# Half of a softmax's row sums as identity products on TensorE, a sorting router, and new orders in a fused adaLN block

## The reference, cut to what matters

```python
h = _rmsnorm(x, norm_w)
v = (h @ W_v.T).reshape(B, T, H, M)                         # H = 8, M = 16
gates = jax.nn.softmax((h @ W_a.T).reshape(B, T, H, M, M + 1), axis=-1)
a0, A = gates[..., 0], gates[..., 1:]
# over the 512 tokens, one after another:
new = jnp.einsum('bhij,bhj->bhi', A_t, state) + (a0 * v)_t
return x + h_out @ W_out.T
```

```python
logits = x @ router_weight.T + router_bias                  # 8 experts
topk_logits, topk_idx = jax.lax.top_k(logits, 4)            # softmax over the four, else 0
act = (clip(up, -7, 7) + 1) * gate * sigmoid(1.702 * gate)  # gate = minimum(gate, 7)
y = sum over experts of combine[expert] * (act @ down_proj.T + bias)
```

## Time and profile before

| | us |
|---|---|
| median of 3 runs | 792.42 |
| the three runs | 788.27, 792.42, 794.17 |
| profiled execution, its own time | 789.0 |
| its span, first to last instruction | 787.3 |
| VectorE busy | 678.0 (86%) |
| TensorE products busy | 589.9 (75%) |
| GpSimd busy | 567.5 (72%) |
| ScalarE busy | 552.2 (70%) |

### The profile page before, as it was taken

One profiled execution on the slowest core, in us unless ns is written; L12 is line 12 of the kernel. 1 busy time (PEld: TensorE's weight loads), 2 busy tenths in 40 slices (PEclk: granted clock), 3 DMA queues, 4 the chain that ended last, 5 costly groups with the idle time before them and its releaser, 6 DMA issues.

```text
span 787.3 us, 12543 instructions
## 1 busy us (share of the span) xinstructions
PE 589.9 (75%) x2826; PEld 441.0 (56%) x2826; DVE 678.0 (86%) x2921; ACT 552.2 (70%) x1272; POOL 567.5 (72%) x635
## 2 busy tenths in 40 slices
PE   5785144787968697877878686979788785878986
PEld 3242022565746475665657474757666574757875
DVE  4569999999999999999999999999989999888331
ACT  4764142777786878787777878786867776657885
POOL 2685556687878797888878787978878686735554
PEclk9886565899999999999999999998989997889998
DMA  6265645453726455364537273644545463720000
GB/s 189 83 145 139 139 116 137 102 130 83 171 79 149 107 122 120 79 159 81 129 95 160 77 159 97 134 115 116 117 79 122 108 141 86 163 71 8 14 8 7
DMA packets 162234, 85.34 MB, mean 108 GB/s; under 512 B 77752, under 2 KB 156784, under 8 KB 157936
## 3 DMA queue, kind: packets, MB, share of 16 engines
q1 hardware_dynamic: 162160, 84.55, 46.3%
HBM read 44.66 MB, written 39.85 MB: 107 GB/s over the span
## 4 chain that ended last, share of the span: by engine, by line
DVE 66%; PE 14%; issue 10%; ACT 5%; POOL 3%; DMA 1%; SPq 1%; POOLq 0%; ACTq 0%; DVEq 0%
DVE ps L854 15%; DVE prod L846 14%; DVE ps L860 8%; DVE act_t L926 7%; DVE nmax L824 6%; DVE zs L831 6%; PE ps L1184 6%; PE ps L1197 4%; DVE rz L837 3%; PE ps L1171 2%; ACT ex L590 1%; ACT ps L624 1%; POOL ex L414 1%; ACT up L618 1%; DMA gates<-gate_dram 1%
## 5 line engine op out<-in xcount | busy, mean ns | idle before, releaser
L1184 PE MATMUL ps<-h2t,wgu 128*128 128x256 f32 x1024 | 256.4, 393 | 24.6 <-ACT up L618 24.6
L1184 PEld LDWEIGHTS ps<-h2t,wgu 128*128 128x128 f32 x1024 | 192.6, 196 | 71.4 <-ACT up L618 29.8
L1171 PE MATMUL ps<-wl,ht 128*128 128x512 f32 (+1 forms) x320 | 168.4, 629 | 71.5 <-ACT lg L601 67.6
L1197 PE MATMUL ps<-wd,act_t 128*128 128x128 f32 x1024 | 146.5, 288 | 65.7 <-DVE act_t L926 65.6
L1197 PEld LDWEIGHTS ps<-wd,act_t 128*128 128x128 f32 x1024 | 135.3, 200 | 95.4 <-DVE act_t L926 84.9
L854 DVE TENSOR_REDUCE ps<-prod 128x8 f32<-128x136 f32 x512 | 152.5, 298 | 10.6
L846 DVE TENSOR_TENSOR prod<-gates,ps 128x136 f32<-128x136 f32 x512 | 147.1, 287 | 14.7 <-DMA gates<-gate_dram 6.4
L421 POOL TENSOR_TENSOR lg<-lg,nmax 128x1088 f32<-128x1088 f32 x64 | 130.3, 2039 | 15.0 <-DVE nmax L824 13.1
L676 ACT ACTIVATE weighted<-ps,comb 128x128 f32<-128x128 f32 x256 | 79.9, 363 | 85.4 <-PE ps L1197 83.1
L461 POOL TENSOR_SCALAR up<-up 128x512 f32<-128x512 f32 x128 | 78.4, 612 | 79.3 <-ACT up L618 75.2
L414 POOL TENSOR_TENSOR ex<-ex,rz 128x1088 f32<-128x1088 f32 x64 | 129.2, 2039 | 8.8 <-DVE rz L837 5.7
(11 more groups left out here) (122 smaller groups left out, 586.0 us busy)
## 6 DMA issues: line engine op xcount, KB each, us to landing
gate_dram<-ex SPq DMA_DIRECT2D x256, 136.0 KB, 3.3
gates<-gate_dram SPq DMA_DIRECT2D x32, 1088.0 KB, 5.5
yt_tok<-y_dram SPq DMA_DIRECT2D x256, 8.0 KB, 3.4
xg<-in_L_attn_x_dram SPq DMA_DIRECT2D x32, 64.0 KB
y_dram<-ys SPq DMA_DIRECT2D x32, 64.0 KB, 2.0
out_dram<-res_out SPq DMA_DIRECT2D x32, 64.0 KB
wa_rows<-in_L_attn_W_a_dram SPq DMA_DIRECT2D x1, 1088.0 KB, 5.7
dn_rows<-in_L_ffn_down_proj_dram SPq DMA_DIRECT2D x1, 1024.0 KB, 12.3
```

The lines of the kernel that those rows point to most:

```text
L1171: nc.tensor.matmul(ps[:, n % 2, 0:w], ht[:, g % RH, j * P:(j + 1) * P], wl[:, k * LC:k * LC + w], start=True, stop=True).then_inc(lg_ps.se ...
L1184: last = nc.tensor.matmul(gu_ps(m, k, which)[:, q * N:(q + 1) * N], wgu[:, k, rows + q * P:rows + (q + 1) * P], h2t[:, m % 2, :], start=Tr ...
L1197: last = nc.tensor.matmul(dn_ps(j), act_t[:, k % 2, q * N + j * P:q * N + (j + 1) * P], wd[:, k, q, :], start=(q == 0), stop=(q == KI - 1))
```

## The change

The row sums of the second tile of a chunk leave VectorE. TensorE adds the 17 columns of every row instead: 17 products with the identity as weights, which accumulate in one of the two banks of the logits; the sum takes one turn among the logits (11 turns for each chunk and not 10). The reciprocal of this tile reads the bank. The product with v no longer waits for the reciprocal's sums on VectorE but for TensorE.

The scan's product leaves out the first column, whose factor was 1, and is written in place over the gates; `prod` and the state's column of ones go. The router sorts the 8 logits (`max`), overwrites the four lower of the sorted list by 2^127, and lets `match_replace` mark the four upper in the logits; its small tensors are in SBUF. `mean_term` goes to GpSimd as a product and a negation. Stores of gates and loads of states are 4 transfers of two batches each. `up`, `act_t` and `weighted` have three buffers. The orders of VectorE's slots, ScalarE, GpSimd and TensorE are changed.

```diff
+        def item_bank(c, i):
+            return ps[:, (ITEMS * c + i) % 2, :]
+        def lg_bank(g, n):
+            return item_bank(g, n if n < SUM_AT else n + 1)          # SUM_AT = 4, ITEMS = 11
+        def zs_bank(e):
+            return item_bank(e + 1, SUM_AT)[:, 0:HI]
...
+            def row_sums(e, part):
+                if part == 0:
+                    wait_item(pe, e + 1, SUM_AT - 2)
+                    pe.wait_ge(exp_ok.sem, exp_ok.at(e, 2))
+                v = ex[:, 1, :].rearrange("p (r k) -> p r k", k=M1)
+                cuts = (0, 6, 12, M1)
+                for k in range(cuts[part], cuts[part + 1]):
+                    last = nc.tensor.matmul(zs_bank(e), ident[:, :], v[:, :, k], start=(k == 0), stop=(k == M1 - 1))
+                if part == 2:
+                    last.then_inc(zs_ps.sem, 1)
...
+                    dve.wait_ge(zs_ps.sem, zs_ps.at(e, 1))
+                    nc.vector.reciprocal(rz[:, j, :], zs_bank(e)).then_inc(rz_ok.sem, 1)
...
-                nc.vector.tensor_tensor(
-                    prod[:, :].rearrange("p (i k) -> p i k", k=M1),
-                    gates[:, t, :].rearrange("p (i k) -> p i k", k=M1),
-                    state[:, (t - 1) % TS, :].unsqueeze(1).broadcast_to([P, HALF, M1]), ALU.mult).then_inc(scan.sem, 1)
+                own = gates[:, t, :].rearrange("p (i k) -> p i k", k=M1)[:, :, 1:M1]
+                nc.vector.tensor_tensor(own, own, state[:, (t - 1) % TS, :].unsqueeze(1).broadcast_to([P, HALF, M]),
+                                        ALU.mult).then_inc(scan.sem, 1)
...
+                elif n == 1:
+                    dve.wait_ge(rank_in.sem, rank_in.at(p, 1))
+                    for j in range(TILES):
+                        nc.vector.max(top[:, j, :], rl[:, j, :]).then_inc(rank_in.sem, 1)
+                elif n == 2:
+                    dve.wait_ge(rank_in.sem, rank_in.at(p, 3))
+                    nc.vector.tensor_tensor(rdl[:, :, :], rl[:, :, :], top[:, :, 0:1].broadcast_to([P, TILES, E]),
+                                            ALU.subtract).then_inc(rank_in.sem, 1)
+                    nc.vector.memset(top[:, :, TOP_K:E], BIG).then_inc(rank_in.sem, 1)
+                else:
+                    for j in range(TILES):
+                        nc.vector.match_replace(out=left[:, j, :], in_to_replace=top[:, j, :], in_values=rl[:, j, :],
+                                                imm_value=-BIG).then_inc(rank_in.sem, 1)
...
+                    nc.vector.scalar_tensor_tensor(out=rsl[:, :, :], in0=left[:, :, :], scalar=-BIG, in1=rex[:, :, :],
+                                                   op0=ALU.is_equal, op1=ALU.mult).then_inc(weigh.sem, 1)
...
+            def mean_term(mv, rs, rs_ok, nm, nx_ok, nm_ok, c):       # in GpSimd's block
+                nc.gpsimd.tensor_tensor(nm[:, :, 0], mv[:, :, 0], rs[:, :, 0], ALU.mult).then_inc(nx_ok.sem, 1)
+                nc.gpsimd.tensor_scalar(nm[:, :, 0], nm[:, :, 0], -1.0, 0.0, ALU.mult, ALU.add).then_inc(nm_ok.sem, 1)
...
-                for b in range(B):
-                    sp.dma_start(gate_dram[j, b // 2, :, b % 2].rearrange("r t e -> t r e"),
-                                 ex[b * TS:(b + 1) * TS, j, :].rearrange("p (r e) -> p r e", e=ROW)
+                for q in range(B // 2):
+                    sp.dma_start(gate_dram[j, q].rearrange("r b t e -> (b t) r e"),
+                                 ex[2 * TS * q:2 * TS * (q + 1), j, :].rearrange("p (r e) -> p r e", e=ROW)
                                  ).then_inc(g_st[j].sem, 16)
```

More of the change, by code:

```diff
@@ L231, in adaln_block @@
         y_st = [event(f"y_st{j}", 16) for j in range(TILES)]
-        y_ld = [event(f"y_ld{j}", 16 * B) for j in range(TILES)]
+        y_ld = [event(f"y_ld{j}", 16 * B // 2) for j in range(TILES)]
         yt_ps, yt_ok, o_ps = event("yt_ps", 1), event("yt_ok", 1), event("o_ps", 1)
@@ L475, in run @@
             def run(a, g, e, s, p, m, o):
+                if o is not None:
+                    finish(o)
+                if m is not None:
+                    clamp_up(m, 0)
                 if a is not None:
@@ L533, in run @@
                     inv_sqrt(ms[:, :, 0], eps_sum, me, rms, me_ok, rms_ok, a)
+                if m is not None:
+                    accumulate(m, 6)
                 if g is not None:
@@ L685, in run @@
                     logits_out(g, 0)
+                if o is not None:
+                    weigh_expert(o, E - 1)
                 if e is not None:
@@ L698, in run @@
                     combine_out(m)
+                    up_and_silu(m, 1)
+                    bias_out(m)
+                if a is not None:
+                    squares(a)
+                if m is not None:
                     weigh_expert(m, 0)
@@ L1033, in between @@
                     if p is not None:
                         second_stats(p, 0)
-                elif u == 57:
-                    if p is not None:
                         second_stats(p, 1)
-                elif u == 59:
+                        for j in range(TILES):
+                            aggregate(st2, mv2, st2_ok, mv2_ok, p, j)
+                elif u == 60:
                     if m is not None:
                         hidden(m, 3)
-                elif u == 60:
-                    if p is not None:
-                        for j in range(TILES):
-                            aggregate(st2, mv2, st2_ok, mv2_ok, p, j)
-                elif u == 66:
+                elif u == 61:
@@ L1067, in between @@
                     if p is not None:
                         router_ranks(p, 0)
-                elif u == 84:
+                elif u == 88:
                     if p is not None:
                         router_ranks(p, 1)
-                elif u == 88:
+                elif u == 91:
                     if p is not None:
                         router_ranks(p, 2)
-                elif u == 89:
+                elif u == 93:
+                    if m is not None:
+                        hidden(m, 7)
+                elif u == 95:
@@ L1260, in run @@
                     logits(g, 0)
+                    logits(g, 1)
                 if m is not None:
                     gate_up(m, 0)
-                if g is not None:
-                    logits(g, 1)
-                if m is not None:
                     gate_up(m, 1)
@@ L1272, in run @@
                     logits(g, 3)
+                if e is not None:
+                    row_sums(e, 0)
+                    row_sums(e, 1)
+                    row_sums(e, 2)
+                if m is not None:
+                    down(m, 0)
+                if g is not None:
                     logits(g, 4)
                 if m is not None:
-                    down(m, 0)
                     down_bias(m)
-                    gate_up(m, 2)
                 if g is not None:
@@ L1285, in run @@
                     gate_up(m, 3)
-                if g is not None:
-                    logits(g, 6)
                 if p is not None:
@@ L1290, in run @@
                 if g is not None:
+                    logits(g, 6)
                     logits(g, 7)
@@ L1293, in run @@
                     down(m, 2)
+                    gate_up(m, 4)
                 if g is not None:
                     logits(g, 8)
+                    logits(g, 9)
                 if m is not None:
-                    gate_up(m, 4)
-                if g is not None:
-                    logits(g, 9)
+                    down(m, 3)
+                    gate_up(m, 5)
                 if a is not None:
@@ L1302, in run @@
                 if m is not None:
-                    down(m, 3)
-                    gate_up(m, 5)
                     down(m, 4)
```

310 lines of the change are left out of this document (123 added, 187 removed).

## The result

The changed kernel takes 863.24 us, the median of four runs (858.91 to 863.94), beside 792.96 for the kernel before (788.27 to 794.17). The ratio is 1.087, with a 95% interval of 1.083 to 1.092: slower by 70 us, where 15 us less was predicted, and far over the range's upper end of 804. Its profiled execution has a span of 861.3 us at a mean granted clock of 0.923; before it was 787.3 at 0.917. They can differ by up to 0.4% from the quotients of the medians printed; that of the kernel before is 790.25 in twelve runs beside the experiments.

What follows compares the result with a forecast made beforehand. VectorE bounds the kernel. Twelve iterations go from 43.16 to 42.2 us, saving 11.5; -11.5 + 1.5 - 1.5 - 1.5 = -13 on the span of 787.3 gives 774.3, as a median 777; range 750 to 804.

Steps and rivals of the forecast that it cites:

- What bounds the kernel: Steady iteration of 42.86 us: VectorE, busy 41.17 in 43 us, sets the pace, with the other engines close behind.
- VectorE's own sum: VectorE's time per steady iteration without new waits for other engines: 42.86 - 2.0 - 0.27 - 0.4 + 0 + 0.3 = 40.5 us.
- locks: Three router instructions of VectorE with two SBUF inputs wait for GpSimd: 1.5 us an iteration, bounds 0 and 4.
- The scan's product and the mean terms: VectorE, per iteration: 128 elements instead of 136 save 0.27 us, mean terms moved to GpSimd save 0.4.
- net 0: Router on VectorE: new small instructions cost 0.6 us an iteration, as the old ones did; bounds -0.3 and +0.8.
- The identity sums: TensorE's 17 products with the identity, 0.22 us each, 3.8 an iteration; the reciprocal at slot 30 waits about 1.
- the identity sums are late: Rival, chance 0.14: stride or low clock doubles the sums' cost on TensorE, giving 806 us.
- Logits(3) starts near 9.4 and ends at 10.2: TensorE's fourth logits product, just ahead of the sums, starts 9.4 us into the iteration, not 10.75; sums end at 14.0.
- The two overlap rather than add: The reciprocal's wait of about 1 us and the locks' 1.5 an iteration overlap, since late locks give TensorE time.
- 42.0 with the locks: Forecast steady iteration: VectorE's own sum of 40.5 us with the locks' 1.5, the reciprocal's wait overlapping.
- a ring of 40: In the 0.14 rival: TensorE and ScalarE's cycle of dependent work, estimated at 40 us; 3.8 more make 44.
- Outside the twelve: Rest of the kernel: two early iterations +1.5 us together, last softmax's iteration -1.5, start -1.5, tail 0.

Runs made afterwards that it cites:

- packed_late: Changed kernel with identity products reading neighbouring elements (stand-in exponentials near 1), router tensors in PSUM, second reciprocal at slot 38: 780.02 us, ratio 0.986.
- lite: Kernel before, in its own orders, with only the 128-element scan product in place and the mean terms on GpSimd: 780.68 us, ratio 0.989.
- ladder: Changed kernel, but identity product k reads its 128 columns with step k + 1, with stand-in exponentials near 1: 856.76 us in one run.
- packed: Changed kernel, but each identity product reads 128 neighbouring elements, with stand-in exponentials near 1: 807.22 us, ratio 1.024.
- nolock: Changed kernel with router logits, marks and masked weights in PSUM, so no router instruction of VectorE reads two SBUF tensors: 842.71 us, ratio 1.067.
- after: The changed kernel itself, with the whole change against the kernel before: 863.24 us, ratio 1.087.
- the whole mended change: Changed kernel, complete, with second-tile exponentials stored in pairs of rows, router tensors in PSUM, second reciprocal at slot 38: 785.47 us, ratio 0.994.

## Why the prediction was wrong

*What bounds the kernel, and VectorE's own sum: right.* The sum of 40.5 shows as 40.8 in packed_late, and its part behind the reciprocal, 40.5 - 13.2 = 27.3, as 27.38 without locks. The scan's product and the mean terms, 0.67 us an iteration, show as 0.6 in lite's shorter iterations and as 0.4 in the mean of its twelve. The two unseen router instructions are cheap: a maximum 155 ns, a match and replace 150 and its load 80, so the router's "net 0" stands, locks apart.

*The identity sums, 17 x 0.22 = 3.8 us: the step that failed.* They took 7.87. The row behind the 0.22, the down products of the earlier trace rows, had neighbouring operands; the new ones step by 17 floats, and by ladder and packed that doubles them. The 3.8 was right for packed (3.96). The prediction named this as the rival "the identity sums are late" and gave it 0.14; of the two reasons it gave there, the stride was the one and the clock was not. Its rows held no strided operand, so they spoke for neither price, and the likeliest sum took the low one as if they had. By the Trainium skill (SBUF — State Buffer, "Door 1: The DMA port swizzle"), accesses are free up to 4 fp32 and cost more beyond; the ladder agrees that a step of 17 costs, but is free only up to 2: 3 costs 1.45 times and 4 already 1.9 times. The page states no price; the doubling in the prediction was its own assumption.

*"Logits(3) starts near 9.4 and ends at 10.2": too early.* The sums begin at 11.1 at best in the steady iterations, without a lock too, where 10.4 was forecast in the same count. TensorE still waits 1.44 us for ScalarE's copies before the fourth logits product (the row at 444.36). These 0.7, and what the lower clock adds to them up to 12.3, were missing; what would bring the copies sooner wasn't tried.

*The locks, 1.5 us within 0 and 4: right in kind, low in size.* 1.39 + 1.1 + 0.4 = 2.9 in the iteration shown, and 2.5 on average over the twelve, since the third lock comes in only three of them. The average over random starts assumed that the three begin at random; but the first took 1.55 us or more in all twelve and the second 1.26 in eleven, in the iteration shown each beside a 2.04 us subtraction of GpSimd, where the prediction itself had put them.

*"The two overlap rather than add": half false.* The two locks ahead of the reciprocal are mostly swallowed by its wait. The one behind it adds its 1.33 each time, and also lengthens TensorE's pause, with which the low clock came twelve times and not seven. In nolock that is worth 20.5 us in all; by the prediction's own terms, 42.0 with the locks and 40.5 + 1.0 without them, it would have been 6.

*The sum.* 42.0 forecast, + 4.1 for the sums' length, + 1.2 for their start (11.6 on average over the twelve, 10.4 forecast), + 0.1 from their end to the reciprocal, + 0.9 behind it (28.7, not 27.8), gives 48.3; 48.36 was measured. The rival's 806 had the doubled price, but assumed an iteration of 44 with a ring of 40; with the late start and the locks it is 48.

*Outside the twelve.* The two early iterations lost 8.2 and not 1.5. Each has one wait, of the reciprocal for the sums; VectorE's timeline after:

```profile
76.42 0.96 DVE L858 RECIPROCAL rz<-ps 128x128 f32<-128x128 f32 x1 [6.13 <-PE ps L1212]
...
118.27 0.96 DVE L858 RECIPROCAL rz<-ps 128x128 f32<-128x128 f32 x1 [6.14 <-PE ps L1212]
```

The wait was forecast as 3, from sums of 5.5 to 7.5 us at a low clock; they took 7.89, and in packed, with neighbouring operands, 5.77 in the second of the two. At the start the four stores issue in 3.50 us instead of the 6.26 of the earlier trace rows, but the first scan product moves only from 58.12 to 57.98: VectorE is now in the experts' weight copies until then, so the transfer was no longer what came last. The last softmax's iteration gained 0.9 (39.2 against 40.2) and not 1.5, the one after it lost 1.0, and the tail lost 3.5 instead of 0; why these two lost wasn't tried and stays open. So does which order of TensorE and ScalarE would let VectorE reach 40.5.

## What to carry to other kernels

Before work moves to TensorE, look at how its moving operand lies: single floats more than two apart cost up to twice. Writing them as columns moved the price to ScalarE, which doubled too, and a later slot for the waiter moved the wait; pairs of neighbours cost little on either engine. Relief of the busiest engine is worth only what the next ring of engines leaves: here two plain edits within the old orders (lite, 1.1%) gave by the medians no less than the whole mended change (0.6%; the two intervals overlap). And cut an iteration at its wait: here a cost ahead of the wait was mostly swallowed, and a cost behind it counted in full.

## What the hardware showed that I had not expected

- TensorE, f32 moving operand of 128 columns at full clock: 0.23 us from start to start at step 1 and 2, 0.33 at 3, 0.44 to 0.47 from 4 to 17. Runs of two with jumps between are nearly free. At half clock neighbours take 0.43 and step 17 still 0.45.
- ScalarE's exponential of 2176 elements: 2.01 us to neighbours, 2.26 with step 2, 3.96 with step 128. GpSimd's product of 1088 elements reads with step 128 in 2.63 us, in pairs in 2.10, in rows in 2.04.
- A clock of 0.50 came with every one of the twelve pauses of TensorE of 3.60 us in after, and with seven of the twelve of 2.27 us in nolock; in the earlier trace rows it was 0.50 after 2.74 us. In the stretches shown, 1.4 us more of VectorE so went with 1.7 us more of TensorE in the next logits products.
- Stores of twice the size (272 KB against 136) land in 4.7 us against 3.3 by the median, and four issue in 3.50 us where eight took 6.26.
